# Scan inputs of two neighbouring states in one GpSimd instruction

## The reference

```
xz = layernorm(layernorm(x)) @ in_proj_w.T     # 512 inner channels for xp, 512 for z
xc = silu(causal_conv4(xp)); dt = softplus(dt_proj(x_proj(xc)))
h[t, d, n] = exp(dt[t, d] * A[d, n]) * h[t-1, d, n] + dt[t, d] * xc[t, d] * B[t, n]
y[t, d] = sum_n h[t, d, n] * C[t, n] + xc[t, d] * D[d]
x = x + glu(gelu((y * silu(z)) @ out_proj_w.T)) + layernorm(x)
```

## Time and profile before

| | |
|---|---|
| time, median of 3 runs | 4621.09 us (4621.03 to 4624.51) |
| span of the profiled execution | 4617.3 us |
| what lies around the span, by the median | 3.8 us |
| POOL busy | 4074.0 us (88%) |
| DVE busy | 3829.4 us (83%) |
| PE busy, weight loads | 3632.1 us (79%), 2285.9 us (50%) |
| ACT busy | 3280.2 us (71%) |
| the 1024 scan inputs on POOL | 2409.4 us |
| the 480 readouts on POOL | 1137.0 us |

### The profile page before, as it was taken

How to read it: one execution, slowest core, us unless ns; L and a number is a source line. 1 busy time by engine, 2 the same in 40 slices (tenths; PEclk the granted TensorE clock), 3 DMA queues, 4 the chain that set the end, 5 groups by cost and what they waited for, 6 DMA issues and landing times.

```text
span 4617.3 us, 56113 instructions
## 1 busy us (share of the span) xinstructions
PE 3632.1 (79%) x16000; PEld 2285.9 (50%) x16000; DVE 3829.4 (83%) x3990; ACT 3280.2 (71%) x4895; POOL 4074.0 (88%) x2223
## 2 busy tenths in 40 slices
PE   3588888888888888888888888888888888876465
PEld 1354555555545555555555545554555454553344
DVE  2899989898989988889989999888989899882433
ACT  3687778787777877878777777787877778772111
POOL 3999999999999999999999999999999999991576
PEclk7798999899999989999989999999989999988666
DMA  3222222222222222222222222222222221220665
GB/s 121 87 75 74 79 80 99 95 99 99 94 100 75 72 66 94 96 98 100 99 95 99 75 72 72 88 99 95 99 99 94 100 75 71 74 77 17 173 158 131
DMA packets 147381, 423.30 MB, mean 92 GB/s; under 512 B 15520, under 2 KB 98656, under 8 KB 113776
## 3 DMA queue, kind: packets, MB, share of 16 engines
q1 hardware_dynamic: 123504, 362.73, 21.3%
q0 software_dynamic: 23552, 56.64, 6.5%
HBM read 333.17 MB, written 52.59 MB: 84 GB/s over the span
## 4 chain that ended last, share of the span: by engine, by line
POOL 39%; issue 22%; DVE 19%; PE 9%; ACT 8%; DMA 2%; POOLq 0%; DVEq 0%; ACTq 0%; SPq 0%
POOL hs L377 19%; POOL hs L386 13%; DVE ps L1165 9%; ACT ps L537 3%; DVE hs L1165 3%; PE ps L884 2%; DVE hs L1175 2%; PE ps L814 2%; DVE xc L1069 2%; POOL dtu L433 2%; PE ps L858 1%; POOL hs L473 1%; POOL rstd L399 1%; DVE xn L1090 1%; ACT L537 1%
## 5 line engine op out<-in xcount | busy, mean ns | idle before, releaser
L377 POOL TENSOR_TENSOR hs<-dtu,b_all 128x1024 f32<-128x1024 f32 x1024 | 2409.4, 2373 | 3.4
L537 ACT ACTIVATE ps<-dt,neg_a 128x512 f32<-128x512 f32 x2048 | 1327.2, 682 | 290.0 <-DVE hs L1175 146.5
L814 PEld LDWEIGHTS ps<-ident,hs 128*128 128x128 f32 x8192 | 1013.9, 151 | 584.9 <-issue 393.3
L1165 DVE TENSOR_TENSOR_SCAN ps<-ps,hs 128x1024 f32<-128x1024 f32 x544 | 1244.2, 2287 | 46.0 <-ACT ps L537 23.8
L814 PE MATMUL ps<-ident,hs 128*128 128x128 f32 x8192 | 1151.4, 290 | 117.3 <-POOL hs L386 75.8
L1165 DVE TENSOR_TENSOR_SCAN hs<-ps,hs 128x1024 f32<-128x1024 f32 x480 | 1088.1, 2278 | 170.2 <-ACT ps L537 147.4
L386 POOL TENSOR_TENSOR hs<-hs,c_all 128x1024 f32<-128x1024 f32 x480 | 1137.0, 2369 | 59.5 <-DVE hs L1165 46.1
L1175 DVE TENSOR_TENSOR hs<-ps,c_all 128x1024 f32<-128x1024 f32 x544 | 665.7, 1224 | 34.4
L924 PE MATMUL ps<-mT,w_sgu 128*128 128x512 f32 x1024 | 522.4, 635 | 12.5 <-DVE hid L1122 9.0
L858 PE MATMUL ps<-xd,w_dt 32*128 32x512 f32 x256 | 185.3, 810 | 234.0 <-ACT dt L609 223.1
L537 ACT ACT_TABLE_LOAD x219 | 281.0, 1283 | 117.3 <-POOL dt L435 113.9
(11 more groups left out here) (127 smaller groups left out, 4448.9 us busy)
## 6 DMA issues: line engine op xcount, KB each, us to landing
b_all<-bc SPq DMA_DIRECT2D x128, 1024.0 KB, 6.0
c_all<-bc SPq DMA_DIRECT2D x128, 1024.0 KB, 7.9
dt<-dtu POOLq DMA_DIRECT2D x64, 512.0 KB, 4.6
table<-rows SPq DMA_DIRECT2D x32, 640.0 KB, 3.8
xin<-x SPq DMA_DIRECT2D x32, 512.0 KB, 3.5
out<-mT SPq DMA_DIRECT2D x32, 512.0 KB, 3.7
c_all<-egu_w SPq DMA_DIRECT2D x64, 256.0 KB, 2.8
c_all<-edown_w SPq DMA_DIRECT2D x64, 128.0 KB, 3.0
```

Of the source, the lines that this page charges most:

```text
L377: pool.tensor_tensor(ring(h, hf, n), dtu[:, JH * hf:JH * hf + JH, :], b_all[:, n, :].unsqueeze(1).broadcast_to([P, JH, L]), ALU.mult)\
L537: i = act.activation(state_of(n)[:, k, :], dt[:, j, :], ACT.Exp, scale=neg_a[:, j, n:n + 1])
L814: m = pe.matmul(ybank[:, i, k * P:(k + 1) * P], ring(h, hf, n)[:, k, i * P:(i + 1) * P], ident[:, :], start=False, stop=(n == N - 1), is_t ...
L1165: dve.tensor_tensor_scan(inputs if s in ON_POOL else whole, whole, inputs, 0.0, ALU.mult, ALU.add).then_inc(state_ready, 1)
```

## The change

`scan_input` becomes `scan_inputs`. It forms the inputs of states n and n + 1 in one instruction of 2048 numbers for each partition: dtu of the half, repeated for two states, times the two rows of B, each repeated for two blocks. The output is two neighbouring slots of the ring. It waits for the sum that frees the second slot, and raises `input_ready` by 2 when the whole instruction is done. POOL calls it at odd steps only, for states s + 3 and s + 4, still ahead of `read_state(s)`. In the prologue it is called for states 0 and 2, so four inputs are formed there and not three.

```diff
-            def scan_input(b, h, hf, n):
+            def scan_inputs(b, h, hf, n):
                 g = b * NS + hf * N + n
+                at = (h * NS + hf * N + n) % HR
                 if n == 0:
                     pool.wait_ge(dt_ready, 4 * b + 2 * hf + 1)
                 if hf == 0 and n % BCN == 0:
                     pool.wait_ge(b_in[n // BCN], 16 * b + 16)
-                wait(pool, summed, g - HR + 1)
-                pool.tensor_tensor(ring(h, hf, n), dtu[:, JH * hf:JH * hf + JH, :],
-                                   b_all[:, n, :].unsqueeze(1).broadcast_to([P, JH, L]), ALU.mult)\
-                    .then_inc(input_ready, 1)
+                wait(pool, summed, g + 1 - HR + 1)
+                pool.tensor_tensor(hs[:, at:at + 2, :, :],
+                                   dtu[:, JH * hf:JH * hf + JH, :].unsqueeze(1).broadcast_to([P, 2, JH, L]),
+                                   b_all[:, n:n + 2, :].unsqueeze(2).broadcast_to([P, 2, JH, L]), ALU.mult)\
+                    .then_inc(input_ready, 2)
...
-                    to = ahead(b, h, s, LEAD, prep)
+                    to = ahead(b, h, s, LEAD, prep) if s % 2 == 1 else None
                     if to:
-                        scan_input(*to)
+                        scan_inputs(*to)
...
-            for n in range(LEAD):
-                scan_input(0, 0, 0, n)
+            for n in range(0, LEAD + 1, 2):
+                scan_inputs(0, 0, 0, n)
```

## The result

The changed kernel takes 4722.4 us (median of 4 runs, 4719.8 to 4736.4) against 4621.1: 1.0233 times the time of before, 95% interval 1.0221 to 1.0245 (the two medians alone give 1.0219). It is slower, as forecast, but by 101 us and not by 24; the range ended at 4675. The span grew from 4617.3 to 4718.0 us.

The account below looks back on a forecast made before the run. POOL was taken to bound stretch P, a DVE-ACT-PE chain stretch V. Boundaries 23.5 us plus stretch P 0 raise the span from 4617.3 to 4640.8; the median lies 3.8 over it: 4645 us, range 4610 to 4675.

Parts of the forecast that it names:

- the two stretches: Each turn is a loop of stretch P, timed by POOL's queue, and stretch V, timed by a DVE-ACT-PE chain.
- stretch P: Step 15 to the memset at step 29, set by POOL: 61.7 us; forecast net change 0 over 30 turns.
- stretch V: Memset to step 15 of the next turn; POOL has spare time, and delays to the chain count in full.
- The saving for a pair: One POOL instruction of 2048 takes 4.54 us against 4.68 for two short ones: 0.14 us saved.
- The boundary: After the memset, scan 0 waits for joined inputs 0 and 1: 15 x 1.15 + 2 x 2.2 + 1.8 = 23.5 us.
- starts of passes: 13 boundaries where ACT stands 2.45 us at the loop's jump, so late scan 0 costs nothing.
- seven savings: Inputs 18 to 31 in stretch P, seven pairs at 0.14 us: 0.97 us less for a turn.
- The new wait for input 20: In stretch P, scan 20 starts 2.0 us late because input 20 ends with 21; readout 22 waits 0.84 us.
- pair 6: In stretch V, the only pair whose stricter wait falls on a recent sum: needed at 2281.3, reached at 2283.5.
- The two ends: The first and last turn add at most 3 us either way.

Follow-up runs that it names:

- pairs_late: Kernel before with pairs only at steps 19, 21, 23, 25 and 27 (inputs 22 to 31), all others short: 4619.5 us, ratio 0.9998.
- singles_0: Changed kernel with the pair of states 0 and 1 issued as two short instructions at the same place: 4696.0 us, 1.0169 of before.
- r15_late: Kernel before, all inputs short, with inputs 18 and 19 both formed at step 15 ahead of readout 15: 4709.8 us, 1.0210 of before.
- r15_late_fill2: r15_late plus two extra PE products at step 17, where PE waits for readout 15: 4650.5 us, 1.0070 of before.
- singles_18: Changed kernel with inputs 18 and 19 as two short instructions at steps 15 and 16: 4691.7 us, 1.0169 of before.
- singles_0_18: Changed kernel with states 0, 1, 18 and 19 as short instructions, all others pairs: 4665.0 us, 1.0096 of before.
- singles_0_18_20: singles_0_18 with states 20 and 21 short too, at their old steps: 4631.7 us, 1.0031 of before.

## Why the prediction was wrong

**The bound, and the two stretches: right.** POOL's work shrank by 69 us and the kernel grew. Both stretches are seen in every kernel of the table. Before, stretch P is within 0.1 us of 61.7 in 28 turns, and not in 30. One part was not right, POOL's spare time in stretch V; it stands under the rest.

**The saving for a pair: right.** 4532 ns measured, 4.54 us estimated; 0.12 us for each pair in `pairs_late` (forecast 0.14).

**The boundary: right in mechanism, and in its total partly by luck.** Of the 15 boundaries in mid-pass, `gate_y` moved by 1.10 to 1.18 us in nine (forecast 1.15 in all), by 1.49 in one and by only 0.2 in five: there PE idled 3.0 us and not 4.2 to 5.3, and its second projection of dt took 1.12 us and not 2.07. So the 15 gave 13.2 us and not 17.3. The two ahead of the loop moved by 2.2 each (forecast 2.2) and the last turn's by 1.06 (forecast 1.8). The 13 starts of passes, forecast at nothing, gave 4.8, most of it in two (1.3 and 2.1). All 31 come to 23.5 us, the number of the forecast, because these misses cancel. `singles_0` takes 26 us back.

**Stretch P: the failed step.** The prediction let seven savings and one new wait cancel: "Over 30 turns, half of each kind, the two cancel: 0 us." They came to +57.4. It counted who waits for the joined inputs, and not who waits for the readouts that were moved behind them. Readout 15 ended 6.56 us after the start of stretch P and now ends at 8.72 on average. PE idled 2.2 to 2.3 us for it, and its clock fell in 23 of 29 turns just ahead of the sum and the logits that DVE needs. That is shown from both sides: by `r15_late`, which loses 92 us against the kernel before with this move alone, in short instructions, and by `r15_late_fill2`, which gets 59 of them back by filling the idling. Where the clock held, the forecast held: 61.6 to 61.7 us in three mid-pass turns of the changed kernel (forecast 61.6), and 62.0 at the starts of three passes (forecast 61.8 to 61.9).

**The new wait for input 20: right, in size too where the clock held.** Forecast 0.84 us for readout 22, and 0.24 more where a pass begins. In the turn whose stretch P starts at 2124.31, scan 20 and readout 22:

```profile
2139.96 2.30 DVE L1167 TENSOR_TENSOR_SCAN ps<-ps,hs 128x1024 f32<-128x1024 f32 x1 [0.41 <-POOL hs L378]
...
2154.25 2.34 POOL L388 TENSOR_TENSOR hs<-hs,c_all 128x1024 f32<-128x1024 f32 x1 [0.78 <-DVE hs L1167]
```

Readout 22 waits 0.78. Scan 20 itself waits 0.41 and not some 2 us, because DVE had already waited 0.87 for the pair of 18 and 19 and 1.09 for PE's sum. `singles_18` has eight turns with a clock of 1.00 both from 6 to 14 and from 20 to 28 us after the start; their stretch P is 61.7 to 61.9 in mid-pass and 62.1 to 62.2 at the starts of passes. Six savings of 0.12 would bring 61.7 to 61.0, so the wait is 0.7 to 0.9 and about 1.1 us, an estimate from these rows (forecast 0.84 and 1.08). The 1.37 between `singles_0_18` and `singles_0_18_20` is larger, because there the clock falls a second time.

**The rest.** From `gate_y` to step 15, 0.40 us for a turn (12 us) were not forecast. Two things are seen there, and neither was tested by itself. Seven of 29 turns before, and four after, took 51.4 us at a mean granted clock of 0.93; the others took 52.7 to 53.7 at 0.88 to 0.91. And POOL does not have time to spare in all of stretch V. Before, it began its chain of step 15 about 0.2 us after DVE's last moment in every turn; after, it began 0.3 to 0.7 us later than that in ten of 29, some 5 us together. On its way it waits for a sum before the pair of 14 and 15 in 31 turns, 52.5 of the 57.3 us that L378's group shows for PE's sums, where the prediction had only pair 6 wait. The two ends cost 8.7 us, and "at most 3" was wrong: 1.1 of it is the boundary of the last turn, and the remainder was not studied. The range was too narrow because it was built from the bounds on the saving, and held no term for a readout that comes late.

The Trainium skill's figure for 2048 numbers ("GPSIMD Engine Reference", section 3.1) was 4497 ns; the trace has 4532, within 1%, and the size of the instruction was never the question. A page of the Trainium skill that bears on what was missed is "TensorE: Matmul & The Clock Gate", Part 1: PE's clock follows how busy PE has been lately. The windows of `r15_late` and `r15_late_fill2` agree: PE busy for 5.25 of 7.70 us at a clock of 0.73, and for 7.03 at 1.00. Why turns of the changed kernel with nearly the same idling went either way stays open.

## What to carry to other kernels

When instructions are joined or moved forward on an in-order engine, list what they are moved past, and who waits for that; the joined work itself may be the smaller part of the loss. Ask of every wait that grows on PE's side what PE does right behind it, because a product that comes after idling may run at half the clock (the logits took 3.52 us here and not 1.90), and what waits for it pays twice. A pair is free only where neither its first half is wanted at once nor a result behind it: of 16 pairs in a turn, three carried 90 of the 101 us.

## What the runs showed of the hardware

- Nearly the same idling had either outcome. In the changed kernel PE's wait for readout 15 was 2.16 to 2.32 us in the six turns in which the clock held and 2.17 to 2.32 in the 23 in which it fell, with 0.68 to 0.85 and 0.80 to 0.98 us of idling shortly before. Some 2 us of stretch P hung on it; what decided is not shown.
- Two calls that compute nothing of use, 1.98 us of PE's time in each turn, made `r15_late` 59 us faster.
- At the loop's jump PE stands for 2.6 to 3.3 us, and the sum behind it took 1.09 us in ten of 13 passes of the kernel before, and 1.96 or 1.97 in seven of those of `pairs_late`.
